# Seams between the stages of a fused vision tower: semaphores, scratch trips and early loads

## The reference

```
h = (patches @ W.T + b, class token first) * pos_embed             # 64 x 65 x 128
h = h + attention(layernorm(h))                                    # 8 heads of 16
x = layernorm(h)
for each of 4 experts:
    g = ln(relu(x @ w1 + b1) @ w2 + b2)                            # width 256
    g = attention(g) @ aow + aob                                   # 16 heads of 16
    mem = concat(lstm_forward(g), lstm_backward(g))                # 65 steps
    gate = sigmoid(relu(mem @ sw1) @ sw2) * tanh(relu(mem @ tw1) @ tw2)
    out[e] = ln(relu(gate @ dw1) @ dw2)                            # width 128
h = h + sum_e softmax(x @ router)[e] * out[e]
```

## Time and profile before

| | us |
|---|---|
| median of 3 runs | 4310.84 (4307.15 to 4312.74) |
| profiled execution, its own time | 4317.09 |
| its span in the profile | 4315.1 |
| PE busy | 3708.7 (86%) |
| DVE busy | 2847.7 (66%) |
| ACT busy | 2158.7 (50%) |
| POOL busy | 1302.4 (30%) |

### The profile page before, as it was taken

The page is one execution under the profiler, slowest core; times in us unless marked ns, Lnnn a source line. Parts: engine busy times, 40 slices in busy tenths (PEclk is TensorE's granted clock), DMA queues, the critical chain, the costliest instruction groups (busy, mean ns, idle before and its releaser), DMA issues. The chain is left out here.

```text
span 4315.1 us, 98606 instructions
## 1 busy us (share of the span) xinstructions
PE 3708.7 (86%) x36068; PEld 2272.8 (53%) x36068; DVE 2847.7 (66%) x5019; ACT 2158.7 (50%) x4389; POOL 1302.4 (30%) x1081
## 2 busy tenths in 40 slices
PE   6769579988988988950999999999999937999997
PEld 4645246645655655630555555555555515666665
DVE  8956448858857857857666666666666653555555
ACT  4536336746755755745444444444444424555554
POOL 0027426726736735735000000000000013444443
PEclk8889779999999989985999999999999967999999
DMA  8910010010010010024111111111111132111121
GB/s 174 174 25 0 40 47 2 0 41 15 0 41 15 0 41 2 0 82 139 46 47 49 49 47 47 49 44 47 47 49 49 47 103 69 52 52 52 52 57 30
DMA packets 393323, 207.22 MB, mean 48 GB/s; under 512 B 151525, under 2 KB 386778, under 8 KB 392410
## 3 DMA queue, kind: packets, MB, share of 16 engines
q1 hardware_dynamic: 393062, 205.29, 18.5%
q10 hardware_dynamic: 116, 0.03, 0.0%
HBM read 147.71 MB, written 57.54 MB: 48 GB/s over the span
## 5 line engine op out<-in xcount | busy, mean ns | idle before, releaser
L1695 PE MATMUL banks<-l_w,l_xs 128*64 128x512 f16 x6240 | 720.9, 381 | 18.1 <-DVE l_xs L1743 17.1
L1695 PE MATMUL banks<-l_w,l_hs 128*64 128x512 f16 x6144 | 705.7, 379 | 1.7 <-DVE l_hs L1749 1.7
L1695 PEld LDWEIGHTS banks<-l_w,l_xs 128*64 128x64 f16 x6240 | 343.8, 110 | 333.4 <-issue 24.4
L1695 PEld LDWEIGHTS banks<-l_w,l_hs 128*64 128x64 f16 x6144 | 348.1, 110 | 316.9 <-DVE l_hs L1749 2.2
L99 POOL MEMSET h_ident<- 128x128 f32 x1 | 0.2, 205 | 1448.1 <-POOLq L76 1448.1
L894 POOL TENSOR_TENSOR ax_p<-ax_p,ax_ri 128x520 f32<-128x520 f32 (+1 forms) x256 | 320.0, 1251 | 270.7 <-DVE ax_ri L1091 270.7
L1801 DVE SCALAR_TENSOR_TENSOR l_gates<-banks,l_unscale,l_bias 128x1024 f32<-128x1024 f32 x260 | 333.7, 1283 | 99.7 <-PE banks L1695 98.2
L1857 ACT ACTIVATE l_gates<-l_gates 128x768 f32<-128x768 f32 x260 | 219.1, 843 | 350.7 <-DVE l_gates L1801 350.7
L2133 PE MATMUL banks<-h_mem,h_w 128*128 128x320 f16 x2496 | 358.4, 300 | 0.0
L865 POOL TENSOR_TENSOR ax_km<-ax_k,ax_mask 128x512 f32<-128x512 f32 x256 | 290.6, 1136 | 14.4 <-PE banks L970 7.4
L2133 PEld LDWEIGHTS banks<-h_mem,h_w 128*128 128x128 f16 x2496 | 245.3, 98 | 93.3 <-issue 0.3
(11 more groups left out here) (299 smaller groups left out, 7238.7 us busy)
## 6 DMA issues: line engine op xcount, KB each, us to landing
image<-in_x_dram SPq DMA_DIRECT2D x192, 196.0 KB
l_x<-x_scratch SPq DMA_DIRECT2D x130, 256.0 KB, 3.0
mem_scratch<-l_hs SPq DMA_DIRECT2D x520, 64.0 KB, 1.9
h_mem<-mem_scratch SPq DMA_DIRECT2D x104, 320.0 KB, 3.7
x_scratch<-x_out SPq DMA_DIRECT2D x4, 4160.0 KB, 16.3
raw_in<-in_L_ffn_attn_in_w_dram SPq DMA_DIRECT2D x4, 768.0 KB, 4.6
h_scratch<-h SPq DMA_DIRECT2D x1, 2080.0 KB, 6.4
z_scratch<-z SPq DMA_DIRECT2D x1, 2080.0 KB, 11.0
```

Of the source, the lines that this page charges most:

```text
L1695: mm = pe.matmul(ps[d * HALF:(d + 1) * HALF, 2 * z + n, :], lhsT, w[:, e, d, kk, b, n * 512:(n + 1) * 512], start=(kk == 0 and turn_ == 0) ...
```

## The change

It has five parts.

1. **Semaphores.** A class `Signals` keeps the semaphores of the stage that is open and of the one before. A new stage has one extra block: in it the five engines clear the semaphores of the stage before, each every fifth, and add `BASE` to those of the new stage, each every fifth. So there are two barriers between the work of two stages instead of three. Fifteen semaphores last through the program and are set up in a block of their own at its start; all that are left are cleared in one block at the end.
2. **Tokens kept.** `Early` holds z, x_out and the expert's raw matrices from the start to the end of the experts. `h` lies in the buffer of `x_out`, and the tokens' `w_rows` in z. n2 stores h and z but does not wait; ACT waits for both (`spilled`) before it first writes to `x_out`. The peaks stay in SBUF. The last save of the tokens is waited for in the LSTM: by ACT before it first writes to `l_w` (which lies over `x_out`), and by SP before it loads tokens.
3. **Matrices early.** A shared `ring` of 2 x 3840 columns serves the experts' normalisation, then three of the LSTM's stage buffers, then two of the head's four. The first expert's matrices are loaded in n2, the first three of the LSTM during the last expert's attention, sets 0 and 1 of the head at the beginning of the LSTM's steps. The head has four buffers, so sets 2 and 3 are loaded at its start without a wait.
4. **Order of transfers.** In the LSTM the tokens of step 0 and the biases stand behind the fifth matrix. In the head the vectors, router and z are issued by ACT, the gains and betas by SP behind sets 2 and 3, with a semaphore of their own (`g_in`) on which DVE waits before it sizes anything.
5. **Smaller tiles.** ACT instead of POOL sorts z in the head, behind set 1. The LSTM's `tc` is its `ig`; the head's work tiles lie in the buffer of set 2.

Core of the diff:

```
+    def open(self):
+        stack, done = self.past
+        with self.nc.Block() as block:
+            on_every_engine(block, done, lambda eng, s: eng.sem_clear(s))
+            on_every_engine(block, self.here[1], lambda eng, s: eng.sem_inc(s, BASE))
+        stack.close()
...
 norm_stage
-                sp.wait_ge(normed, BASE + WSTEPS)
-                sp.dma_start(spill[0], src[:, :]).then_inc(spilled, 16)
-                sp.dma_start(spill[1], dst[:, :]).then_inc(spilled, 16)
-                sp.wait_ge(spilled, BASE + 32)
+            early.load(sp, experts_io, 0, shared.raw_loaded)
+            sp.wait_ge(normed, BASE + WSTEPS)
+            sp.dma_start(h1_dram, h[:, :]).then_inc(shared.spilled, 16)
+            sp.dma_start(z2_dram, z[:, :]).then_inc(shared.spilled, 16)
...
 experts_stage
-            load(0)
-            sp.dma_start(z[:, :], z2_dram).then_inc(z_in, 16)
...
+            sp.wait_ge(h_ready, BASE + EXPERTS * STEPS)
+            for q in range(3):
+                load_lstm_matrix(sp, io, q, shared.stage(q), shared.stage_in[q])
             save(EXPERTS - 1)
-            sp.wait_ge(peaked, BASE + EXPERTS * att.UNITS)
-            sp.dma_start(peak_dram, peak[:, :]).then_inc(saved, 16)
-            sp.wait_ge(saved, BASE + 16 * (EXPERTS + 1))
...
+                act.wait_ge(shared.spilled, BASE + 32)
...
 lstm_stage
-        tc = sb("l_tc", [P, D])
+        tc = ig
...
+                if q == STAGES:
+                    sp.wait_ge(shared.x_saved, BASE + 16 * EXPERTS)
                     load_x(sp, 0, 0)
-                if q == STAGES - 1:
                     for e in range(EXPERTS):
...
+            sp.wait_ge(w_low, BASE + MATRICES)
+            for e in range(2):
+                load_head_matrices(sp, io, e, shared.ring[:, e * RAW:(e + 1) * RAW], shared.head_in[e])
...
-            for e in range(EXPERTS):
-                sp.wait_ge(saved[e], BASE + SEQ * 32)
...
+                if q == 0:
+                    act.wait_ge(shared.x_saved, BASE + 16 * EXPERTS)
...
 head_stage
+            for e in range(2, E):
+                load_head_matrices(sp, io, e, raw[e], raw_in[e])
             for e in range(E):
-                sp.dma_start(gain[:, e, :], io["dec_g"][e].partition_broadcast(P)).then_inc(v_in, 16)
-                sp.dma_start(beta[:, e, :], io["dec_beta"][e].partition_broadcast(P)).then_inc(v_in, 16)
+                sp.dma_start(gain[:, e, :], io["dec_g"][e].partition_broadcast(P)).then_inc(g_in, 16)
+                sp.dma_start(beta[:, e, :], io["dec_beta"][e].partition_broadcast(P)).then_inc(g_in, 16)
...
+            for e in range(2):
+                sp.wait_ge(shared.saved[e], BASE + SEQ * 32)
+                load_mem(0, e)
...
-                if e == 2:
-                    pool.wait_ge(z2_in, BASE + 16)
-                    pool.tensor_copy(z2s[:, 0:SEQ, :], major(h1[:, :])).then_inc(z2_sorted, 1)
...
+            dve.wait_ge(g_in, BASE + 32 * E)
...
+                if e == 1:
+                    act.wait_ge(z2_in, BASE + 16)
+                    act.copy(z2s[:, 0:SEQ, :], major(h1[:, :])).then_inc(z2_sorted, 1)
```

More of the change, by code:

```diff
@@ new lines, in on_every_engine, with _ @@
+def on_every_engine(block, signals, do):
+    @block.sync
+    def _(sp):
+        for s in signals[0::5]:
+            do(sp, s)
+    @block.gpsimd
+    def _(pool):
+        for s in signals[1::5]:
+            do(pool, s)
+    @block.tensor
+    def _(pe):
+        for s in signals[2::5]:
+            do(pe, s)
+    @block.vector
+    def _(dve):
+        for s in signals[3::5]:
+            do(dve, s)
+    @block.scalar
+    def _(act):
+        for s in signals[4::5]:
+            do(act, s)
@@ L1566, in lstm_stage @@
         sb = lambda name, shape, dt=F32: ctx.enter_context(nc.sbuf_tensor(name, shape, dt))
-        sem, made = semaphores(nc, ctx)
+        sem = signals.stage()
         ident = sb("l_ident", [P, P])
-        ones = sb("l_ones", [3, P])
-        peak = sb("l_peak", [P, EXPERTS, UNITS])
-        w = sb("l_w", [P, EXPERTS, 2, 2 * KD, 2, G4], F16)
+        spare = lambda rows, at, n: shared.ring[0:rows, 3 * KD * G4 + at:3 * KD * G4 + at + n]
+        ones = spare(3, 0, P)
+        peak = shared.peak
+        w_of = [sb("l_w0", [P, 2, 2 * KD, 2, G4], F16)]
         bias = sb("l_bias", [P, EXPERTS, G4])
@@ L1602, in lstm_stage @@
                                     "h_done", "turned", "h_high", "h_low")]
-        saved = [sem(f"l_saved{e}") for e in range(EXPERTS)]
-        block = open_block(nc, ctx, made)
+        saved = shared.saved
+        block = open_block(nc, ctx, signals)
         SIZING = 11
@@ L1903, with head_stage @@
 NHEAD = 13
-def head_stage(nc, ps, io, h1_dram, z2_dram, mem_dram, out):
+def head_stage(nc, signals, shared, ps, io, h1_dram, z2_dram, mem_dram, out):
     TC = 5
@@ L2496, in vit_tower, with stages @@
     x = scratch("x_scratch", EXPERTS, SEQ, P, KD, IMAGES)
-    peak = scratch("peak_scratch", P, EXPERTS * IMAGES // GROUP)
     mem = nc.dram_tensor("mem_scratch", (EXPERTS, 2, SEQ, P, 2, KD, IMAGES), F16).ap()
-    with nc.psum_tensor("banks", [P, 8, 512], F32) as ps:
-        stages(nc, ps, first, experts, inputs, h1, z2, x, peak, mem, out)
-def stages(nc, ps, first, experts, inputs, h1, z2, x, peak, mem, out):
-    front(nc, ps, {key: inputs[name] for key, name in first.items()}, h1, z2)
-    experts_stage(nc, ps, experts, z2, x, peak)
-    lstm_stage(nc, ps, experts, x, peak, mem)
-    head_stage(nc, ps, experts, h1, z2, mem, out)
+    with nc.psum_tensor("banks", [P, 8, 512], F32) as ps, ExitStack() as ctx:
+        signals = Signals(nc, ctx)
+        stages(nc, signals, ctx, ps, first, experts, inputs, h1, z2, x, mem, out)
+def stages(nc, signals, ctx, ps, first, experts, inputs, h1, z2, x, mem, out):
+    shared = Shared(nc, ctx, signals)
+    with ExitStack() as until_lstm:
+        early = Early(nc, until_lstm)
+        front(nc, signals, shared, early, ps, {key: inputs[name] for key, name in first.items()}, experts, h1, z2)
+        experts_stage(nc, signals, shared, early, ps, experts, x)
+    lstm_stage(nc, signals, shared, ps, experts, x, mem)
+    head_stage(nc, signals, shared, ps, experts, h1, z2, mem, out)
+    with nc.Block() as block:
+        on_every_engine(block, shared.made + signals.here[1], lambda eng, s: eng.sem_clear(s))
+    signals.here[0].close()
 _FFN = ("router_w router_b enc_w1 enc_b1 enc_w2 enc_b2 enc_g enc_beta attn_in_w attn_in_b attn_out_w attn_out_b "
```

249 lines of the change are left out of this document (126 added, 123 removed).

## The result

The changed kernel took 4261.82 us (median of 4 runs, 4250.56 to 4264.3), the kernel before 4311.69 in the same session (4307.15 to 4312.74): a ratio of 0.9877, 95% interval 0.9865 to 0.9888, 49.9 us less. 4248 was predicted, within 4230 to 4272. The profiled execution took 4262.6, which is 54.5 less than that of the kernel before, where the sum had 62.5.

A forecast was written before the change was run, and what follows sets the result against it. No engine was taken as the bound at a seam, but all five standing still and a new stage's time to its first product. Gains of 5.2, 17.8, 14.9, 22.0 and 2.6 sum to 62.5 us: 4248 us, range 4230 to 4272.

The forecast's parts named there:

- The seam's price: Between stages: 0.056 us per semaphore operation on any engine, as on SP; the six seams take 0.85 to 1.5 us.
- The 0.056: Seams between stages: us per semaphore operation on SP, fitted on two seams of the kernel before and checked on two.
- C: All seams: sharing semaphores among five engines is no quicker than SP; 20.8 us lost, gain 41.7, 4269 us; chance 0.09.
- Norm to experts: Second norm to the experts' first ACT step: no wait for spills, no reload of z; 17.8 us gained.
- rival A: Whole kernel: small loads land only with the stream in front of them; gain 48.5 us, 4262; chance 0.20.
- Experts to LSTM: Last tokens to first LSTM product: stage 20.4 us sooner, 5.5 given back behind the bias loads; net gain 14.9 us.
- B: Loads are free: gains at 3508.1, DVE not held at fourth sizing, matrix six hidden; gain 76.2 us, 4235; chance 0.15.
- LSTM to head: LSTM's last issue to the head's first product: 1.6 us from an earlier first sum, 20.4 from a shorter chain; 22.0 gained.
- The 23 us: Head's start to DVE's first sum, held by the gain and beta loads; taken near the upper end because bytes set it.
- D: LSTM steps: the product waits for the tile shared with tanh of the cell; 109 us added, 4357; chance 0.04.
- Inside the stages: Within all stages: same products, activations and reductions in the same order, nothing that carries time changed; no gain or loss.
- The median: Whole kernel: the profiled execution of before lies 6.25 us above the runs' median, so 4254.6 on its scale becomes 4248.

The follow-up runs named there:

- e1_sp_only: Changed kernel with all semaphore clears and additions on SP alone instead of shared among five engines, still two barriers; 4285.51 us, ratio to before 0.9937.
- e4_z_later: Changed kernel with SP's store of z moved into the experts' stage, once the expert's vectors have landed; 4257.44 us, ratio to before 0.9871.
- e3_by_rate: Changed kernel with semaphores shared by each engine's own pace per operation, so that all five end together; 4263.1 us.
- e5_bias_last: Changed kernel with the LSTM's 24 bias loads behind the last matrix instead of ahead of matrix six; 4250.67 us, ratio to before 0.9862.
- e7_z_on_pool: Changed kernel with the head's sorting of z back on POOL instead of ACT; 4266.88 us, ratio to before 0.9894.
- e6_gain_last: Changed kernel with DVE's wait for gains and betas behind its four sizings, and ACT waiting for the LSTM's last saves before its first cast; 4255.23 us, 0.9866.

## Why the prediction was right, and where 8 us were missing

**The seam's price** is the step that failed: "I take SP's price, since nothing nearer is there". There was something nearer. The barriers of the kernel before hold a semaphore operation on each engine, and the trace has their durations:

```profile
L76 SPq EVENT_SEMAPHORE  x1: 17/17/17, 3496.9 to 3496.9; - x1
...
L76 DVEq EVENT_SEMAPHORE  x1: 21/21/21, 3496.9 to 3496.9; - x1
L76 PEldq EVENT_SEMAPHORE  x1: 51/51/51, 3496.9 to 3496.9; - x1
```

51 ns against 17: PE could be seen to take three times as long (from one addition to the next it is 2.6 times SP's), and an equal share is then set by PE. The 0.056 itself, fitted on two seams of SP and checked on two more, was right (e1_sp_only: 60 operations more, 84 against 24, cost 3.37 us, 0.056 each). The six seams came out 6.3 us longer than forecast and the end 0.6. C, that five engines are "no quicker than on SP", was wrong as a whole (e1_sp_only has the seams 10.4 us longer) and right in part of its reason, "several times slower per operation": PE is, the three others take 1.2 to 1.6 times as long as SP.

**Norm to experts**, 14.1 instead of 17.8. The 7.0 us to the transpose were 9.2: they "ran beside 3.4 MB on SP's queue" before, and the forecast took such company to be the same as the two stores. e4_z_later shows that it isn't. This is rival A at this place: the vectors landed with the stores, at 528.6 behind 528.06 (A had 2.2 us for it, it was 3.7). Since the stores and not the seam set that time, e3_by_rate's shorter seam gave nothing; its stores landed 1.1 us later after their issue, and ACT's first step came 1.2 us later behind the norm. So the 3.7 us missing here are the vectors', and the seam's own 1.5 lie hidden in them. The Trainium skill, DMA: Bandwidth & Descriptors, Queues, rings and completion order, has the completion of a DMA behind every earlier write of that engine on any queue. The rows agree: the transpose keeps 0.6 to 0.7 us behind z's landing, also in e3_by_rate, where it comes 4.3 us behind the last issue instead of 2.7. Whether the slower issue (up to 1.22 us for a load instead of 0.32) adds anything to that is not shown, since e4_z_later took away both at once.

**Experts to LSTM**, 13.9 against 14.9, with the steps as told: pairs at 24.8, 48.8 and 62.2 us of the stage where 25.4, 49.2 and 62 stood, the waits for save and biases included. The stage's own length grew by 5.15 us (122.77 to 127.92), "5.5 us go back"; the rest is the seam. What the prediction undervalued is the alternative: B gave 5.5 us for matrix six hidden, since it measured against the pace of before; e5_bias_last gave 9.7.

**LSTM to head**, 20.9 against 22.0: first sum at 23.2 us (23), chain 67.1 (68), seam 3.4 (1.5). Of the chain's 21.3 us less, 5.8 are POOL's copy gone (e7_z_on_pool); that no sizing waits for a load is the likely rest, which no run took apart. The 23 us were right in kind as well, though not step by step: 13.6 us of issue were 19.2, one load of set 3 alone taking 5.4. They rested on bytes that DVE's sizing doesn't need: the wait cost 9.8 us by e6_gain_last, and B's lower bound gave 5.2.

**LSTM steps, tc and ig**: unchanged, D is out. **Inside the stages** "nothing is changed that carries time": true of the instructions, but the experts alone vary by 15 us with the clock, which is more than any term that was missed. It hid behind a sum that came out at -0.3 us here, because 5.2 us less in the early stages stood against 5.5 more in the experts. That is luck.

**The median.** The prediction took 6.25 us off because the profiled execution lay that far above the median; by the later runs that of before lay 5.4 above its own, that of the changed kernel 0.8. Such a distance belongs to one execution. 7.9 us of terms, 0.3 of stages and 5.5 of this distance are the 13.8 us from 4248 to 4261.8, to within rounding. The 4262 of rival A is met by chance only: of its terms the vectors' alone came true, the first sum stood at 23.2 us of the head where A had about 28, and the pairs and the LSTM's steps were not later.

## What to carry to other kernels

A seam is worth shortening only where the next stage's first need is already there: ask which transfer, issued before the seam, is waited for behind it, and put small loads ahead of big stores. Share work among engines by what one operation takes on each, not by count. And ask of each wait at a stage's start whether the instruction behind it reads what is waited for, but also what else the wait happens to protect.
